# Layer-1 messages kept in DRAM instead of an on-chip ring, eight tiles of gathered rows instead of four, and 24 batches gathered beside the copy instead of 20

## What is computed

```python
h = relu(layernorm(x))
x = x + L0(h)            # sums of weighted neighbour rows, scaled by degrees
h = relu(layernorm(x))
x_i = h[dst]; x_j = h[src]
feat = concat([x_i, x_j - x_i])            # 25000 x 512
msg  = relu(feat @ W1 + b1) @ W2 + b2      # 512 -> 512 -> 256
x = x + segment_sum(msg, dst) / (deg + 1e-8)
```

## Time and profile before

| | |
|---|---|
| median of three runs | 2137.04 us |
| the profiled execution | 2144.27 us |
| its span | 2142.5 us |
| TensorE / VectorE / ScalarE / GpSimd busy | 81% / 70% / 48% / 60% of the span |
| granted TensorE clock, mean | 0.912 |
| longest groups on GpSimd | layer-1 gathers 409.6 us (x400), layer-1 scatters 328.1 us (x200) |

### The profile page before, as it was taken

How to read it: one execution, slowest core, us unless ns; L and a number is a source line. 1 busy time by engine, 2 the same in 40 slices (tenths; PEclk the granted TensorE clock), 3 DMA queues, 4 the chain that set the end, 5 groups by cost and what they waited for, 6 DMA issues and landing times.

```text
span 2142.5 us, 46594 instructions
## 1 busy us (share of the span) xinstructions
PE 1731.1 (81%) x14020; PEld 1512.9 (71%) x14020; DVE 1496.0 (70%) x6002; ACT 1031.7 (48%) x2106; POOL 1289.5 (60%) x1024
## 2 busy tenths in 40 slices
PE   6957888887667666720599999999999999999992
PEld 2257878786666665720598988988888888788882
DVE  8968888987666766720577777777777676777661
ACT  0024444444333333410467676676757565666651
POOL 2033223378888888865434334488888888888864
PEclk9979999998887878865799999999999999999996
DMA  8999999656566656645999999955555555555543
GB/s 288 317 303 327 322 338 324 208 103 110 99 104 103 105 104 103 99 55 112 325 336 332 332 338 333 331 96 93 95 92 97 93 96 93 97 92 97 94 70 37
DMA packets 142803, 379.84 MB, mean 177 GB/s; under 512 B 31805, under 2 KB 97352, under 8 KB 129864
## 3 DMA queue, kind: packets, MB, share of 16 engines
q0 software_dynamic: 86400, 131.14, 34.9%
q1 hardware_dynamic: 27452, 208.63, 27.4%
q10 hardware_dynamic: 28912, 39.64, 7.2%
HBM read 325.72 MB, written 259.17 MB: 273 GB/s over the span
## 4 chain that ended last, share of the span: by engine, by line
POOL 23%; DMA 12%; issue 12%; SPq 6%; POOLq 0%
POOL table_out L932 12%; POOL ends L920 11%; DMA table_out<-x 10%; SPq L907 6%; DMA table_out<-e_ring,e_targets_all 2%; SPq L903 0%; SPq L902 0%; POOLq L930 0%; POOLq L941 0%; POOLq L928 0%; POOLq L968 0%
## 5 line engine op out<-in xcount | busy, mean ns | idle before, releaser
L920 POOL DMA_INDIRECT ends<-x,keys x400 | 409.6, 1024 | 308.0 <-PE ps_h L1244 108.7
L772 PE MATMUL ps_deg<-table,hot 128*128 128x128 bf16 x5600 | 358.6, 226 | 75.3 <-issue 52.7
L772 PEld LDWEIGHTS ps_deg<-table,hot 128*128 128x128 bf16 x5600 | 336.2, 101 | 92.5 <-issue 83.2
L465 POOL DMA_INDIRECT x<-sums_ring,targets_all x200 | 329.9, 1649 | 89.4 <-issue 65.6
L932 POOL DMA_INDIRECT table_out<-e_ring,e_targets_all x200 | 328.1, 1641 | 91.6 <-issue 57.5
L455 POOL DMA_INDIRECT rows<-in_x,row_idx x200 | 208.1, 1040 | 248.0 <-ACT normed L699 193.9
L1244 PE MATMUL ps_h<-feat_hi,w_hi 128*128 128x512 f32 x800 | 320.8, 401 | 12.0 <-DVE feat_lo L1061 7.4
L1244 PE MATMUL ps_h<-feat_hi,w_lo 128*128 128x512 f32 x800 | 316.8, 396 | 0.0
L1244 PE MATMUL ps_h<-feat_lo,w_hi 128*128 128x512 f32 x800 | 316.7, 396 | 0.0
L786 PE MATMUL ps_sum<-msg_hi,same 128*128 128x260 f32 x800 | 157.5, 328 | 157.9 <-issue 151.4
L786 PEld LDWEIGHTS ps_sum<-msg_hi,same 128*128 128x128 f32 x800 | 133.8, 230 | 163.0 <-issue 162.9
(11 more groups left out here) (141 smaller groups left out, 3521.4 us busy)
## 6 DMA issues: line engine op xcount, KB each, us to landing
table_out<-x SPq DMA_DIRECT2D x400, 252.0 KB
x<-in_x SPq DMA_DIRECT2D x400, 250.0 KB
hi_row<-hi_rows ACTq DMA_DIRECT2D x50, 256.0 KB
src_row<-src_rows ACTq DMA_DIRECT2D x50, 256.0 KB
dst_row<-dst_rows ACTq DMA_DIRECT2D x50, 256.0 KB
ends<-x,keys POOLq DMA_INDIRECT x400
rows<-in_x,row_idx POOLq DMA_INDIRECT x200
x<-sums_ring,targets_all POOLq DMA_INDIRECT x200
```

What stands on the lines that cost most here:

```text
L465: pool.indirect_dma_start(out=x1_d, out_offset=bass.IndirectOffsetOnAxis(ap=targets_all[:, b, j:j + 1], axis=0), in_=sums_ring[:, b % RING ...
L772: last = nc.tensor.matmul(ps_deg[q][k][:, j * P:(j + 1) * P], hot[:, c, k, j * P:(j + 1) * P], table[:, c, part, :], start=(c == 0 and par ...
L920: pool.indirect_dma_start(out=ends[b % NE][:, n, :], out_offset=None, in_=x1_d, in_offset=bass.IndirectOffsetOnAxis(ap=keys[:, 1 - end, at ...
```

## The change

Layer 1's sums no longer stay on chip until they are scattered. ScalarE writes each batch's scaled sums into one of two tiles `e_sums` and issues a DMA of 512 KB that writes them to the DRAM tensor `sums_d` (`keep`). SyncE, after all pieces of the copy have been issued, reads each batch back into one of BACK = 6 tiles `back`; from the seventh on a read waits until the batch six before it has been scattered. POOL's scatter waits for that read instead of for `e_in_ring`, and its scatters take `back` as source.

The tiles of gathered rows become eight (NE = 8; the loops of all engines then run over eight batches, and ScalarE's starts eight batches later). LEAD1 is 24. `pace` is a formula: the gathers of batches 2 to 23 are spread over the processing of batches 0 to 15. After the copy 208 gathers are left, put between the scatters as 5 per 2 half batches: two after a batch's first half, three after its second.

```diff
-    RING1 = 20
-    NE = 4
+    BACK = 6
+    NE = 8
-    LEAD1 = 20
+    LEAD1 = 24
+    sums_d = nc.dram_tensor("sums_d", (NB, P, W * D), fp32).ap()
...
-            e_ring = sb("e_ring", [P, RING1, W, D], fp32)
+            e_sums = [sb(f"e_sums{q}", [P, W, D], fp32) for q in range(2)]
+            back = [sb(f"back{k}", [P, W, D], fp32) for k in range(BACK)]
...
@@ sync, behind the loop of the copy
+                for b in range(NB):
+                    sp.wait_ge(kept[b % 2], 16 * (b // 2 + 1))
+                    if b >= BACK:
+                        sp.wait_ge(back_free, b - BACK + 1)
+                    sp.dma_start(back[b % BACK][:].rearrange("p j d -> p (j d)"), sums_d[b, :, :])\
+                        .then_inc(back_in[b % BACK], 16)
@@ gpsimd
                 def scatter(b, g):
-                    pool.wait_ge(e_in_ring, GROUPS * (b + 1) + g + 1)
                     if g == 0:
+                        pool.wait_ge(back_in[b % BACK], 16 * (b // BACK + 1))
                         pool.wait_ge(e_target_ready, b + 1)
                     for j in range(G * g, G * g + G):
                         pool.indirect_dma_start(
                             out=out, out_offset=bass.IndirectOffsetOnAxis(ap=e_targets_all[:, b, j:j + 1], axis=0),
-                            in_=e_ring[:, b % RING1, j, :], in_offset=None, compute_op=ALU.add)\
+                            in_=back[b % BACK][:, j, :], in_offset=None, compute_op=ALU.add)\
                             .then_inc(e_scattered, 16)
...
                     if g == GROUPS - 1:
-                        pool.sem_inc(e_ring_free, 1)
+                        pool.sem_inc(back_free, 1)
+                STEPS = 4 * (LEAD1 - NE)
+                PAIRS = W * (LEAD1 - 2)
                 def pace(b, n):
...
+                    elif b == 2 and n == 0:
+                        pool.wait_ge(ends_in[1], 16 * 2 * W)
+                    elif b >= 2:
+                        step = (W * (b - 2) + n // 2) * STEPS // PAIRS
+                        c, k = step // 4, step % 4
+                        if k < 2:
+                            pool.wait_ge(mm1_done, KH * c + 2 * k + 2)
                         else:
+                            pool.wait_ge(mm2_done, GROUPS * c + k - 1)
...
                     scatter(c // GROUPS, c % GROUPS)
-                    for n in range(min(left, 11 * c // 4), min(left, 11 * (c + 1) // 4)):
+                    for n in range(min(left, 5 * c // 2), min(left, 5 * (c + 1) // 2)):
                         gather(LEAD1 + n // (2 * W), n % (2 * W))
                     scatter_end(c // GROUPS, c % GROUPS)
@@ scalar
+                def keep(b, q):
+                    act.wait_ge(e_scaled, GROUPS * (b + 2))
+                    act.dma_start(sums_d[bass.ds(b, 1), :, :].rearrange("o p w -> (o p) w"),
+                                  e_sums[q][:].rearrange("p j d -> p (j d)")).then_inc(kept[q], 16)
...
-                        last = nc.scalar.activation(e_ring[:, bass.ds(b % RING1, 1), j, :], ps_s[g][:, a * D:(a + 1) * D],
+                        last = nc.scalar.activation(e_sums[q][:, j, :], ps_s[g][:, a * D:(a + 1) * D],
                                                     ACT.Copy, scale=inv_deg[q][:, j:j + 1])
```

More of the change, by code:

```diff
@@ L877, in gnn_preln_two_layers @@
             e_summed = sem("e_summed")
-            e_in_ring = sem("e_in_ring")
-            e_ring_free = sem("e_ring_free")
+            e_scaled = sem("e_scaled")
+            kept = [sem(f"kept{q}") for q in range(2)]
+            back_in = [sem(f"back_in{k}") for k in range(BACK)]
+            back_free = sem("back_free")
             e_scattered = sem("e_scattered")
@@ L908, in _ @@
                                      x1_flat[bass.ds(FLIGHT * r + k, 1)]).then_inc(bulk_out[k], 16)
+                for b in range(NB):
[4 more added lines that the diff above has]
+                        .then_inc(back_in[b % BACK], 16)
             @block.gpsimd
             def _(pool):
-                pool.sem_inc(e_ring_free, RING1)
                 def gather(b, n):
@@ L947, in pace @@
                         pool.wait_ge(ends_in[0], 16 * 2 * W)
[L948 to L952, removed]
-                        else:
[L954 to L959, removed]
+                    elif b == 2 and n == 0:
[5 more added lines that the diff above has]
+                            pool.wait_ge(mm1_done, KH * c + 2 * k + 2)
+                        else:
+                            pool.wait_ge(mm2_done, GROUPS * c + k - 1)
                 for b in range(LEAD1):
@@ L1035, in after_of @@
                     dve.wait_ge(e_deg_done, b + 1)
-                    dve.wait_ge(e_in_ring, GROUPS * b)
+                    dve.wait_ge(e_scaled, GROUPS * b)
                     nc.vector.reciprocal(inv_deg[q][:], deg_eps[:]).then_inc(inv_deg_done, 1)
@@ L1115, in _ @@
                     for n in range(1, NE + 1):
-                        step(NE * i + n, 2 * i + n // 2, n % 2, n % NE, i + n // NE)
+                        step(NE * i + n, NE // 2 * i + n // 2, n % 2, n % NE, i + n // NE)
                 for b in range(NE * QUADS + 1, NB):
@@ L1122, in _ @@
                 act.sem_inc(e_normed_done, 2)
-                act.sem_inc(e_in_ring, GROUPS)
+                act.sem_inc(e_scaled, GROUPS)
                 def load_keys(b, q):
@@ L1165, in out_high, with scale @@
                                          ACT.Copy).then_inc(out_hi_done, 1)
-                def scale(b, q, g):
+                def keep(b, q):
+                    act.wait_ge(e_scaled, GROUPS * (b + 2))
+                    act.dma_start(sums_d[bass.ds(b, 1), :, :].rearrange("o p w -> (o p) w"),
+                                  e_sums[q][:].rearrange("p j d -> p (j d)")).then_inc(kept[q], 16)
+                def scale(b, t, q, g):
                     act.wait_ge(e_summed, GROUPS * (b + 1) + g + 1)
-                    act.wait_ge(e_ring_free, b + 1)
+                    if g == 0 and not (isinstance(b, int) and b < 2):
+                        act.wait_ge(kept[q], 16 * t)
                     act.wait_ge(inv_deg_done, b + 1)
-                    act.sem_inc(waited, 1)
                     for a in range(G):
                         j = G * g + a
-                        last = nc.scalar.activation(e_ring[:, bass.ds(b % RING1, 1), j, :], ps_s[g][:, a * D:(a + 1) * D],
+                        last = nc.scalar.activation(e_sums[q][:, j, :], ps_s[g][:, a * D:(a + 1) * D],
                                                     ACT.Copy, scale=inv_deg[q][:, j:j + 1])
-                    last.then_inc(e_in_ring, 1)
+                    last.then_inc(e_scaled, 1)
                 def step(b, t, q, u, v, last=False, load=True):
@@ L1197, in step @@
                         if not first(b):
-                            scale(b - 1, 1 - q, g)
+                            scale(b - 1, t - 1 + q, 1 - q, g)
                         out_high(b, g)
+                    if not first(b):
+                        keep(b - 1, 1 - q)
                     if load:
@@ L1208, in _ @@
                     feat_high(0, k)
-                step(*whole(0))
-                with act.Fori(0, QUADS) as i:
+                for b in range(NE + 1):
+                    step(*whole(b))
+                with act.Fori(1, QUADS) as i:
                     for n in range(1, NE + 1):
-                        step(NE * i + n, 2 * i + n // 2, n % 2, n % NE, i + n // NE)
+                        step(NE * i + n, NE // 2 * i + n // 2, n % 2, n % NE, i + n // NE)
                 for b in range(NE * QUADS + 1, NB):
@@ L1215, in _ @@
                 for g in range(GROUPS):
-                    scale(NB - 1, 1, g)
+                    scale(NB - 1, (NB - 1) // 2, (NB - 1) % 2, g)
+                keep(NB - 1, (NB - 1) % 2)
             @block.tensor
@@ L1265, in sums @@
                         pe.wait_ge(out_lo_done, GROUPS * b + g + 1)
-                        pe.wait_ge(e_in_ring, GROUPS * b + g + 1)
+                        pe.wait_ge(e_scaled, GROUPS * b + g + 1)
                         for a in range(G):
```

## The result

| | before | after |
|---|---|---|
| median | 2136.98 us (4 runs, 2134.32 to 2138.99) | 2161.46 us (4 runs, 2157.76 to 2164.79) |
| ratio to before | 1 | 1.0103, 95% interval 1.0082 to 1.0123 |
| the profiled execution | 2144.27 us | 2159.45 us |
| its span | 2142.5 us | 2157.7 us |

The change costs 24.5 us where +30 was forecast (2167 us). The sum came out nearly right, but by luck: of its two large errors one was too much and the other too little, and they nearly cancel.

The account below looks back on a forecast made before the run. The DMA engines were taken to bound layer 1 until the copy's end, then POOL. Terms of -32 + 46.5 + 3 + 0 + 12 made +29.5, say +30 us: 2167 us, range 2140 to 2200.

Parts of the forecast that it names:

- case (A): The forecast itself: the copy is pushed back by more than POOL saves, 2146 to 2200 us; chance 0.74.
- Part 1: POOL after the copy: 208 gathers instead of 240 leave fewer halves with three, a gain of 32 us (28 to 33).
- Part 2: Copy's end: 32 more gathers 15.5 us, 16 writes 29, two more `dst_row` loads 2; 46.5 us later (40 to 52).
- the 25 at which I wanted to call the prediction fallen: Copy's end: the prediction was to fall if it moved by less than 25 us.
- rival (B): Copy: other traffic fits between its pieces, so it ends only 5 to 10 us later; 2122 us, faster; chance 0.10.
- The other count, 13.1 MB: Copy's delay counted by bytes instead: 13.1 MB more at 335 GB/s, 39 us + 2.
- The 31 us estimated from them: Copy's delay if 13.1 MB passed at the skill page's 425 GB/s; whole change then some 15 us lower.
- Part 3: Reads back on chip: POOL's first scatter waits for read 0 after the copy, 3 us (0 to 8); later no wait.
- Part 4: Layer 1's start: TensorE, VectorE and ScalarE some 10 us later, hidden under the copy with 45 us to spare; cost 0.
- Part 5: Scatters after the copy: writes and reads delay their landing, mostly in halves with two gathers; 12 us (0 to 45).
- Rival (C): Scatters: every first half meets the read in full, 71 us instead of 12; 2226 us; chance 0.07.
- the signs that I named: New profile: first scatter 1436 to 1448 us, first to last scatter 715 to 725, halves with two gathers near 6.7.

Follow-up runs that it names:

- both transfers small: The changed kernel with DRAM writes of the sums and reads back of 64 KB instead of 512 KB, most messages left out; ratio 0.9966 to the kernel before.
- last ring version: Kernel before with on-chip ring of 16, six tiles, 22 batches beside the copy, batch 2 gathered early, 224 gathers left as 2 and 3 per half; ratio 0.9927, 2132.29 us.
- The ring version: Kernel before with on-chip ring of 16, six tiles, 22 batches beside the copy at the changed kernel's pace, 224 gathers over 90 halves; ratio 0.9977.
- the run with four tiles: The changed kernel with four tiles and the old lead, pace and interleave, so only the sums' way through DRAM is new; ratio 1.0176, 2187.61 us.
- the run with eight tiles: Sums through DRAM with the old lead, pace and interleave, but eight tiles and loops over eight batches instead of four; ratio 1.0232, 2193.3 us.
- second pair: Kernel before and changed kernel profiled once more on another chip with no edit; ratio 1.0126.

## Why the prediction was right, and where its steps failed

The copy and then POOL bound layer 1, and the two costs, of the copy and of the collisions, exist with the sign that I gave. The time lies in the range and in case (A). That it lies so near the forecast is luck. By steps:

- **Part 1, 32 us by fewer gathers.** The prices 6.6 and 7.9 us held nearly where the traffic was small (6.83 and 7.87 us with both transfers small). What failed is that all of it could be had. TensorE's last sums came at about 1102 us in the best cases, and the last scatter then at 1112.1 us with the ring and at 1124.1 with both transfers small, against 1127.1 before: 15 and 3 us of gain, not 32. In the changed kernel itself this limit wasn't reached: its last scatter starts 36 us behind its last sums (2111.0 to 2146.7).
- **Part 2, the copy 46.5 us later.** Measured 25.7 and 28.6 us for the copy's end, just over the 25 at which I wanted to call the prediction fallen. The term that failed is the engine time. I took a write at 1.8 us between bounds of 1.46 and 2.1; it is 1.2 to 1.3 us, below the lower bound. And I added 0.485 us for each gather to a copy that kept its own price, while a piece of it went from 0.712 to 0.686 us, 10 us over 400 pieces. The 16 more gathers of the last ring version moved the copy's end from 388.0 and 390.6 to 388.6 us, the 32 with both transfers small by 4 to 7. A share of 0.99 with 335 GB/s was no ceiling: the mixes reached 348 GB/s at 0.98. The mechanism of rival (B) was there in part, for the gathers, but not for the writes, which cost 1.2 to 1.3 us each. (The other count, 13.1 MB, holds the two loads already if 16 writes are meant, so its "+ 2" counts them twice.) The 425 GB/s of the Trainium skill's page "HBM Reference" (section "Specifications") were not reached from 1100 to 1350 us in any of these runs. The 31 us estimated from them are nearer to the measured 26 and 29 than my 46.5, but the highest of these stretches had 350 GB/s, so this doesn't bear the figure out.
- **Part 3, 3 us.** First scatter 3.7 and 3.1 us after the end of the copy, 1.5 before, so 2 us where I said 3. After the first scatter POOL never waited for `back`. When the ring began to empty before, 16 of its 20 places were filled, not the 17 that I gave.
- **Part 4, the start 10 us late, no cost.** First sums 84.6 us after the first gather instead of 73.7: right, and hidden under the copy here, by less than I said: POOL's last gather beside it came 15 and 23 us before the copy's end, not 45. The last sums, which I had at 2095 us, came at 2111.0, in layer 1's time 27 us later than that, since they followed the last gather by 69 us and not by 50; POOL was still 36 us behind them. The ring version showed what it costs without that cover.
- **Part 5, 12 us of collisions.** Measured 30 us in the first profile. I bounded it by loads of layer 0, and took the cover of 0.4 and 1.4 us as if a landing came late by little each time. It comes late seldom and by much, up to 4 us when a write, a load and a read meet, and then the 1.4 us in halves with three gathers don't cover it either: they too lost 0.22 us on average. The messages alone explain 20 of the 30 us, as the run with four tiles shows. Rival (C), the whole read in each first half, was not seen (7.03 us, not 8). What makes the other 10 stays open. I left out what the loops' length does, but the 6 us of the run with eight tiles don't prove it. The ring versions, and the kernel with both transfers small, lie 11 us over the old prices too, with little or no message traffic.

Together: forecast -32 + 46.5 + 3 + 12 = +29.5. In the first pair of profiles the first scatter is 27.8 us later, the scatters' stretch 1.5 us shorter: +26.3 us, and +34.5 in the second pair (30.2 + 4.3), beside 24.5 and 27 us by the medians. The forecast was near because part 2 was 18 to 21 us too high and part 5 18 to 23 us too low. Of the signs that I named, the first scatter (1436 to 1448 us; 1410.7 and 1425.5) and the stretch (715 to 725 us; 736.0 and 741.0) were both missed, and so was the half with two gathers (near 6.7 us; 7.0). The 236 pieces of the copy, the longer waits for landings and the late first sums came as said.

## What to carry to other kernels

A detour through DRAM costs twice: the writes lengthen whatever already fills the DMA engines, and reads and writes delay small transfers whose landing someone waits for. It is worth it only for what the freed memory buys. Here six tiles, a ring of 16 and a pace that doesn't delay the start had that gain without leaving the chip. Price the transfers in the stretch where they run, and before you count a saving on one engine, look how far ahead of it the next one ends.

## What the runs showed of the hardware

DMA engines that were 0.99 busy at 335 GB/s took more traffic at 348 GB/s and 0.98: here the queues' shares didn't add up to a fixed price per transfer. A write of 512 KB from 128 partitions cost 1.2 to 1.3 us of all 16 engines, less than its bytes at the rate of the DRAM to DRAM copy beside it (1.46 us at 358 GB/s, 1.41 at 371). Two scatters of 128 rows landed 3.8 us after the second one's start when they were alone, and 8.19 us after it when a write, a load and a read fell on them. The kernel with loops over eight batches in place of four had 135 packets on the instruction queues instead of 39, and pauses of TensorE of up to 4.0 us.
